# A graph layer in one kernel: score rows computed early, attention maxima moved among the product tiles, and input rows normalized in spans of 4, 4 and 2 tiles

## What is computed

```python
xn = layernorm(x)
# 1. two graph attention convolutions (4 heads of 192, then 2 heads of 96)
h = layernorm(xn) * g + b;  h = h @ W1           # the "first attention product"
s_src, s_dst = (h * a_src).sum(-1), (h * a_dst).sum(-1)      # the scores, per node and head
e = leaky_relu(s_src[src] + s_dst[dst], 0.2)
ee = exp(e - segment_max(e, dst)[dst])
out = segment_sum(ee / segment_sum(ee, dst)[dst] * h[src], dst) + bias
# 2. linear attention with exponential features of keys and queries of xn
# 3. x = x + [x, out2] @ Wu + bu + mix(xn), then a mixture of 8 experts, top 2
```

## Time and profile before

| | us |
|---|---|
| median of 3 runs | 1347.99 |
| the three runs | 1347.99, 1320.34, 1348.22 |
| the profiled execution | 1314.55 |
| its span, first to last instruction | 1312.8 |
| TensorE busy | 1092.2 (83%) |
| VectorE busy | 816.8 (62%) |
| ScalarE busy | 401.0 (31%) |
| GpSimd busy | 306.4 (23%) |

### The profile page before, as it was taken

The page is one execution under the profiler, slowest core; times in us unless marked ns, Lnnn a source line. Parts: engine busy times, 40 slices in busy tenths (PEclk is TensorE's granted clock), DMA queues, the critical chain, the costliest instruction groups (busy, mean ns, idle before and its releaser), DMA issues.

```text
span 1312.8 us, 15580 instructions
## 1 busy us (share of the span) xinstructions
PE 1092.2 (83%) x6105; PEld 975.1 (74%) x6105; DVE 816.8 (62%) x1648; ACT 401.0 (31%) x522; POOL 306.4 (23%) x227
## 2 busy tenths in 40 slices
PE   2999956999999992018999794678699999999998
PEld 1898535667899992018888794677569999999998
DVE  7558993107632595978999668697935433454344
ACT  2443010334100214017666331672242221222211
POOL 1157888888883400010000000000000000000000
PEclk8999985999999996558999897798899999999999
DMA  6926652423555804012000002001010111011103
GB/s 205 312 47 157 127 102 14 72 1 50 118 117 57 238 18 138 0 41 81 1 1 0 1 22 99 0 1 49 1 48 1 48 48 49 1 48 49 49 0 118
DMA packets 67241, 83.14 MB, mean 63 GB/s; under 512 B 31419, under 2 KB 50189, under 8 KB 67169
## 3 DMA queue, kind: packets, MB, share of 16 engines
q1 hardware_dynamic: 37601, 62.27, 15.2%
q0 software_dynamic: 29568, 19.89, 10.1%
HBM read 67.59 MB, written 14.54 MB: 63 GB/s over the span
## 4 chain that ended last, share of the span: by engine, by line
PE 60%; DVE 26%; issue 7%; DMA 3%; ACT 3%; POOL 1%; DVEq 0%; SPq 0%; ACTq 0%; POOLq 0%
PE bank L1280 51%; PE bank L1482 7%; DVE junk_m L1060 7%; DVE junk_k L929 6%; DVE pbuf L1131 3%; DVE pbuf L1105 3%; PE bank L1291 2%; ACT vbuf L762 1%; DVE h L1114 1%; DMA cnt<-table 1%; DVE sb_stats L876 1%; DVE x L1180 1%; DVE sb_stats L877 1%; ACT pbuf L771 1%; DMA keyrow<-key_d 1%
## 5 line engine op out<-in xcount | busy, mean ns | idle before, releaser
L549 POOL DMA_INDIRECT table<-match_n,slot_ix x168 | 277.6, 1652 | 89.6 <-issue 49.7
L1482 PE MATMUL bank<-h,pbuf 128*128 128x193 f32 (+1 forms) x1200 | 190.2, 319 | 31.5 <-DVE pbuf L1131 30.4
L1482 PEld LDWEIGHTS bank<-h,pbuf 128*128 128x128 f32 x1200 | 181.6, 197 | 40.1 <-DVE pbuf L1131 35.9
L1280 PE MATMUL bank<-f_hi,hT 128*128 128x384 f32 x640 | 167.4, 336 | 0.0
L1280 PEld LDWEIGHTS bank<-f_hi,hT 128*128 128x128 f32 x640 | 117.0, 189 | 0.6
L1211 DVE TENSOR_TENSOR hT<-silu,hT 128x512 fp32r<-128x512 f32 (+1 forms) x48 | 28.8, 603 | 141.4 <-ACT hT L825 141.3
L1262 DVE SCALAR_TENSOR_TENSOR x<-bank,sb_gate,x 128x384 f32<-128x384 f32 x160 | 93.5, 613 | 28.9 <-PE bank L1280 28.6
L1280 PE MATMUL bank<-f_lo,hT 128*128 128x384 f32 x320 | 107.7, 337 | 0.0
L1280 PE MATMUL bank<-y2T_hi,f_hi 128*128 128x512 f32 (+1 forms) x288 | 103.2, 358 | 2.9 <-DVE y2T_lo L860 2.9
L929 DVE SCALAR_TENSOR_TENSOR junk_k<-keyrow,key,sb_before 128x384 uint8<-128x384 f32 x168 | 92.8, 614 | 20.1 <-DMA keyrow<-key_d 20.1
L1280 PE MATMUL bank<-y2T_lo,f_hi 128*128 128x512 f32 (+1 forms) x288 | 102.9, 357 | 0.0
(11 more groups left out here) (244 smaller groups left out, 1992.3 us busy)
## 6 DMA issues: line engine op xcount, KB each, us to landing
keyrow<-key_d SPq DMA_DIRECT2D x28, 384.0 KB
table<-zero POOLq DMA_DIRECT2D x2, 3201.0 KB, 28.4
cnt<-table POOLq DMA_DIRECT2D x20, 320.0 KB, 10.9
f_raw<-in_w1T SPq DMA_DIRECT2D x8, 768.0 KB, 4.8
f_raw<-in_w2T SPq DMA_DIRECT2D x8, 768.0 KB, 6.3
w_raw<-in_kqvT SPq DMA_DIRECT2D x4, 1152.0 KB, 7.1
acc_d<-ubuf SPq DMA_DIRECT2D x20, 192.0 KB, 2.1
u_row<-m_d POOLq DMA_DIRECT2D x6, 640.0 KB, 7.8
```

Of the source, the lines that this page charges most:

```text
L549: pool.indirect_dma_start(table[i], bass.IndirectOffsetOnAxis(ap=slot_ix[:, g:g + 1], axis=0), match_n[:, g:g + 1], None, compute_op=ALU.a ...
L1280: return nc.tensor.matmul(o, l, r, start=first, stop=last)
L1482: ins = nc.tensor.matmul(b[:, d * stride:d * stride + chans + 1], score[:, dt * P:(dt + 1) * P], h_t[:, st, h, 0:chans + 1], start=st == 0 ...
```

## The change

- **Spans.** Rows are normalized in spans of 4, 4 and 2 tiles; TensorE turns the second span after key product 0 and the third after key product 2. ScalarE's third square root stands after `channels` of product 2.
- **Second statistics.** Mean 0 and variance `var * rs1 * rs1` are used in place of new `bn_stats`; that root is begun after chunk 1 and used after chunk 12.
- **Loads.** A table gives slot, weights and last use. W1 is loaded whole near the start; key rows 0 and 1 are loaded before the second key half; the 24 small loads of `wk` and `wq` become 6. GpSimd zeroes the tables as soon as x is in, from 388 elements of 16 bits a piece in place of 1067, and table 0 starts at 128 in every entry, so that a count can be read as a bf16 number.
- **Score rows.** `wa` = W1 by `a_src` and `a_dst`: 48 short `tensor_tensor_reduce` on VectorE, three in each of the chunks 3 to 18. In the `u` stage TensorE forms the scores of all nodes from it (`score_rows`, 54 matmuls, bank `sc`) after `bias_rows(0)`, then `score_columns` and `scT`. The 80 `dots` of the `h1` stage and the row_sums go.
- **G copies** and the blocks made from `kvt` and `ksT` move to ScalarE.
- **h1 stage.** ScalarE takes each `h1` tile out (one operation). The low half of W1 is made with g in one operation per block (`split_gain_lo`, 6 short ones). TensorE turns `cnt` itself (no `edge` copy), one mask tile after each of the h1 tiles listed in `PEN_AT`. VectorE runs `masked_max` for mask tiles 0 to 3 with all heads, then tiles 4 to 9 head by head, with `leaky_max` and a transposed row (`max_rows`) for each head. ScalarE takes 128 off `cnt` at the end.
- **Rows of head 0** are loaded like the others; `spread_row` of head 0 goes.

```diff
-        LOADS = [(kT, 0), (kT, 1), (vT, None), (projT, None), (qT, 0), (qT, 1), (Wu[0:D, :], 0), (Wu[0:D, :], 1), (W1, 0), (W1, 1)]
+        LOADS = [(2, kT, 0, None), (1, kT, 1, None), (0, W1, None, None), (2, vT, None, ("k", 0, 2, 2)),
+                 (0, projT, None, None), (1, qT, 0, ("k", 1, 2, KD - 1)), (2, qT, 1, ("kvt",)),
+                 (0, Wu[0:D, :], 0, ("M", 2, 1)), (1, Wu[0:D, :], 1, ("q", 2, KD - 1)),
+                 (2, W1, 0, ("q", 2, KD - 1)), (1, W1, 1, ("u", 1, NT - 1))]
...
+        SPANS = [range(4), range(4, 8), range(8, NT)]
+        SPAN_AT = {0: SPANS[1], 2: SPANS[2]}
...
+        PEN_AT = [(0, 1), (0, 2), (0, 3), (0, 4), (1, 0), (1, 1), (1, 2), (1, 3), (1, 4), (1, 5)]
+        ROWS_AT = {(1, 6): 0, (1, 9): 1}
...
             for c in range(NCH):
                 compare_chunk(c)
                 if c == 1:
                     split_half_lo(dve, K0 + 1)
-                    for t in range(NT):
-                        tile_stats(xrow, t, mv2)
-                    inv_std(mv2, rs2)
+                if c == 1:
+                    step(nc.vector.tensor_tensor(mv2[:, :, 1], mv[:, :, 1], rs1[:, :], ALU.mult))
+                    step(nc.vector.tensor_tensor(mv2[:, :, 1], mv2[:, :, 1], rs1[:, :], ALU.mult))
+                    inv_std_begin(mv2)
...
+                if 3 <= c < 19:
+                    for k, j, h in dot_list[3 * (c - 3):3 * (c - 2)]:
+                        step(nc.vector.tensor_tensor_reduce(
+                            out=junk_d[:, :], in0=w1[:, k, h * C1:(h + 1) * C1], in1=(accb, row_t)[j][:, h * C1:(h + 1) * C1],
+                            scale=1.0, scalar=0.0, op0=ALU.mult, op1=ALU.add, accum_out=wa[:, k, j * H1 + h:j * H1 + h + 1]))
...
+                if c == 20:
                     split_half_lo(dve, Q0)
...
+                    if (hf, t) == (0, 3):
+                        bias_rows(0)
+                        score_rows()
+                    if (hf, t) == (0, 5):
+                        score_columns()
...
                     ins.then_inc(full("h1", hf, t), 1)
-            pe.wait_ge(dots_done, 1)
...
+                    if (hf, t) == (0, 0):
+                        bias_rows(1)
+                    if (hf, t) in PEN_AT:
+                        mask_tile(PEN_AT.index((hf, t)))
+                    if (hf, t) in ROWS_AT:
+                        max_rows(ROWS_AT[hf, t])
+            max_rows(2), max_rows(3)
```

On SP, behind the last stores of the `u` stage:

```diff
+            evacuated(sp, "scT")
+            sp.wait_ge(s_out, 16)
             for i in range(UR):
                 sp.wait_ge(u_out[i], 16 * (2 * NT // UR))
...
+            for h in range(H1):
+                sp.dma_start(a_row[h][:, :], row_of(s_d, h)).then_inc(a_in[h], 16)
+            load_weights(A0 + 1)
```

More of the change, by code:

```diff
@@ L138, in gps_layer @@
         h1 = at("h1", 61440, [P, NT, H1, S1])
[L139 to L144, removed]
@@ L153, in gps_layer @@
[L153 to L157, removed]
+        cnt = [at(f"cnt{i}", SL[0] + 2560 * i if i < 7 else EARLY + 2560 * (i - 7), [P, T], U16) for i in range(NT)]
+        ident_b = at("ident_b", SL[0] + 17920, [P, P], BF16)
@@ L255, in gps_layer @@
                 reserve("kf", *K_MAIN[j - 1])
+            for t in SPAN_AT.get(j, ()):
+                reserve("xT", t, 0), reserve("xT", t, 1)
         reserve("kf", *K_MAIN[-1])
@@ L454, in _ @@
                 if i == UR:
[L455 removed]
+                    load_weights(A0)
                 if i >= 3:
@@ new lines, in _ @@
+            act.wait_ge(rs2_done, 1)
+            for hf in range(2):
+                for t in range(NT):
+                    h1_out(hf, t)
+                    if hf == 0 and t == 3:
+                        split_gain_hi(act, A0 + 1)
+                        weight_rows(1)
+                    if (hf, t) in PEN_AT:
+                        dt = PEN_AT.index((hf, t))
+                        if dt == 4:
+                            finished(act, "h1", 0, NT - 1)
+                        if dt == 0:
+                            for i in range(UR):
+                                act.wait_ge(u_out[i], 16 * (2 * NT // UR))
+                        mask(dt, 0), mask(dt, 1)
@@ L745, in rows_out @@
+            for i in range(NT):
+                nc.scalar.activation(cnt[i][:, :], cnt[i][:, :], ACT.Identity, bias=less_c[:, 0:1]).then_inc(cnt_done, 1)
             def rows_out(stage, k, h, row):
@@ L906, in x_lo @@
                         lo_part(xnT[1][s], transposed(psum("xT", t, h), h), xnT[0][s], "xT", t, h)
-            for tiles in (range(NT // 2), range(NT // 2, NT)):
+            for tiles in SPANS:
                 for t in tiles:
@@ L941, in compare_chunk @@
                                         trash_c[:, :].unsqueeze(1).broadcast_to([P, 2, KW]), ALU.add).then_inc(slots_done, 1)
+            w1 = whole[SLOT[WA]]
+            dot_list = [(k, j, h) for k in range(KD) for j in range(2) for h in range(H1)]
             for c in range(NCH):
@@ L968, in _ @@
-            sums = b[:, 0:MH * M].rearrange("p (g f) -> p g f", g=3)
-            for a in range(4):
-                r = slice(M * a, M * (a + 1))
-                ins = nc.vector.tensor_copy(KD_[r, :, r], sums[r, :, r])
-                ins.then_inc(free("ksT"), 1) if a == 3 else step(ins)
             split_half_lo(dve, Q0 + 1)
@@ new lines, in max_rows, with mask_tile @@
+            def max_rows(h):
+                pe.wait_ge(m_done, h + 1)
+                b = take(pe, "mT", h)
+                nc.tensor.transpose(b[0:2 * NT, 0:P], ucol[:, h, :, :].rearrange("p k t -> p (k t)"), ident[:, :]).then_inc(full("mT", h), 1)
+            def mask_tile(dt):
+                if dt == 0:
+                    pe.wait_ge(cnt_diag, NT)
+                    pe.wait_ge(ident_done, 1)
+                for j in range(2):
+                    b = take(pe, "pen", dt, j).bitcast(BF16)
+                    for i in range(5):
+                        ins = nc.tensor.transpose(b[:, i * P:(i + 1) * P], cnt[5 * j + i].bitcast(BF16)[:, dt * P:(dt + 1) * P],
+                                                  ident_b[:, :])
+                    ins.then_inc(full("pen", dt, j), 1)
```

592 lines of the change are left out of this document (332 added, 260 removed).

## The result

The changed kernel takes 1281.82 us (median of 4 runs, 1281.1 to 1283.0). The kernel before, run beside it, took 1320.1, 1320.3, 1348.0 and 1348.2; its runs fall into two groups some 28 us apart, and the comparison uses the faster one. The ratio is 0.971, with a 95% interval of 0.969 to 0.973. The forecast was 1269, with a range of 1234 to 1302.

A forecast was written before the change was run, and what follows sets the result against it. TensorE, busy for 83% of the span, was taken as the bound, its waits as what can be won. Attention 51.4 us sooner took the span from 1312.8 to 1261.4, execution 1263, plus 5.8 gave 1269 us; range 1234 to 1302.

The forecast's parts named there:

- Step 1: Start of the kernel: key product 0 some 15 us sooner, 4.4 us gained at the end of key features and G.
- Step 2: Wait for G: ScalarE copies G, leaving a 1.2 us wait for the first query half; TensorE's shift becomes -30.6 us.
- Step 3: u stage: 6.6 us wait for the first W1 half, scores added, row_sums gone; shift -10.8 us, ending at 417.45.
- Step 4: Second bias row, behind the first h1 tile: second W1 half lands at 433.15, TensorE waits 12.6 us, bounds 7.4 to 15.5.
- the paragraph on cover: GpSimd's scatters end at 389 and table reads at 411, before TensorE asks at 440; a cover of 29 us.
- Steps 5 and 6: h1 tiles with masks until 502.95, then three more heads' maxima; first attention matmul at 542.8 in place of 594.2.
- The stretch from attention on: From the first attention matmul to the end: left as it is, 718.6 us.
- A: Both W1 halves land in time, without a stall; 27.6 us given back, 1241 us; chance 0.18.
- B: Tables or first query half late, through zeroing, scatters or dots; costs 20 to 25 us, 1292 us; chance 0.16.
- D: VectorE's maxima don't get in among the h1 tiles; gain only about 25 us, 1295 us; chance 0.12.
- C: TensorE stays at its lower clock from the first W1 wait to the last mask; 1350 us and more; chance 0.04.
- The 5.8 us added to the profiled execution: Added to the summed 1263 us because the earlier kernel's profiled execution lay 5.8 below its lowest run; gives 1269.

The follow-up runs named there:

- experiment 6: Changed kernel, one part undone each: all spans ahead of key product 0, 1281.53 us; odd G copies on VectorE, 1283.85; masks behind last h1 tile, 1312.45.
- experiment 3: Changed kernel with the last 24 of 168 scatters left out: 1256.19 us.
- experiment 5: Changed kernel with the 254 filling edges given distinct pairs of unused nodes in place of one repeated pair: 1264.96 us, ratio to before 0.963.
- Experiment 6, third part: Changed kernel with all ten mask tiles and the turns of the maxima behind the last h1 tile: 1312.45 us.
- experiment 8's last kernel: Changed kernel with distinct filling nodes, second W1 half sent ahead of the score rows, its bias row behind h1 tile 3, split behind tile 4: 1247.0 us.
- experiment 4: Changed kernel with the second W1 half's bias row behind h1 tile 6 in place of tile 0, split behind tile 7: 1307.14 us.

## Why the prediction was right, and where it was off

- **Step 1, the start: right.** The first query product, directly behind the key features and `G`, starts at 170.37 in place of 173.47: 3.1 us gained, 4.4 forecast. (The 9 us of experiment 6 are measured against another order, which is slower than the kernel before.) Product 0 came 15.5 us sooner (15 forecast), and the waits of the later spans were 1.2 and 2.9 (3 and 3 forecast).
- **Step 2, `G`: right.** Shift -32.3 for -30.6. The 1.2 us that I had for the first query half did not appear, the products behind `G` took 17.1 us in place of 20.8 (2 had been put down for the clock), and experiment 6 shows that the wait hangs on the copies.
- **Step 3, `u`: right.** The half landed at 321.3 (321.0 forecast); the wait was 8.93 for 6.6 because TensorE came 2.0 us earlier. The stage's shift is -11.1 for -10.8.
- **Step 4, the second W1 half: this one failed.** "So 417.45 + 3.4 + 12.3 = 433.15. TensorE waits 12.6 us." The row shows 34.94. The half landed 22.1 us late. Its first term, 3.4 us from the last `u` tile to the last landed store, measured 8.4; its second, 12.3 us for the rows and the half behind them, measured 29.8. The mechanism of the queue was right: with the slow stretch away the second term is 12.8 (experiment 3) or 12.6 (experiment 5), and the wait 12.3 or 16.4. What failed is the paragraph on cover, "168 of them end at 389, and 20 table reads (about 22 us) at 411". They were sent from 420.2 to 436.9 and landed until 460, over the half's flight. So the load shared the DMA engines with them, which the sum had put at nothing. I had priced the scatters by their pitch on GpSimd, and not by when the last had landed, though the row of `cnt` in the same group, 431.64, could not tell it: there the reads waited for the stores of `u`.
- **Steps 5 and 6, `h1`, masks, heads: right.** From the second bias row to the first attention matmul 106.9 us (forecast 542.8 - 433.15 = 109.7), with the wait of 4.1 for a bank (forecast 4) and heads at a pitch of 10.6. Experiment 6, third part, prices the overlap at 31.9 us.
- **The stretch from attention on: right**, 716.6 for 718.6.
- **Rivals.** A (no stall) is refuted. B did not come by its own sign, a TensorE that waits for `cnt`, nor by its causes, the zeroing or the dots. But the tables were late, complete at 460 in place of 411: the cover that was held against B was not there, and it showed as a longer wait for the half. B's price of 20 to 25 us fits. D did not come. C gave no loss in this kernel beyond the restarts in the sum: the bias rows took 6.61 and 6.23 us, where the second takes 4.03 in experiment 8's last kernel, which has no wait before it. But the mechanism exists, elsewhere: experiment 4 loses 32.9 us to a stage that stays at 1.2 GHz. The Trainium skill (TensorE: Matmul & The Clock Gate, A second HAM failure mode: psum-queue depth-cycling) warns of small idle gaps between groups that throttle the array again and again. What the windows show is unlike it: no gap at all, 8.00 us busy in each 8.00, and the clock low throughout.
- **The 5.8 us added to the profiled execution** had no mechanism, and the changed kernel does not show them: its profiled execution, 1281.1, is 0.7 below the median. That they brought the forecast nearer is luck: the steps alone gave 1263, 18 us too low. The range, drawn to hold D's 1295 as well, held a half that came 22 us late.

The missing 17 us of the span are 22.1 from step 4, less 2.8 from what follows it and 2.0 behind the first attention matmul. Step 4 also explains why undoing the gains of steps 1 and 2 cost so little: until edit 5 the second bias row starts at 454.6, 455.2 or 458.8, whether TensorE comes to it at 429.9, 420.3 or 443.3. What sets it in the first two is GpSimd's chain, scatters, their slow end and the table, which TensorE does not move; only from about 440 on does TensorE's own end of `u`, with the last store and the load behind it, become the later one.

What stays open: why adds onto 256 neighbouring bytes hold up stores of another queue (that they do is shown, not how, and the adds' own packets stay short), and what decides whether TensorE comes back to 2.4 GHz before the `w2` products.

## What to carry to other kernels

When a change moves the busy engine forward, look for the chain that does not move with it, here GpSimd's scatters, and date it by landings, not by sendings: a queue that was never waited for can be 20 us slower than it looks. If undoing a part of a change costs nothing, look at the next wait before calling the part useless: it may have shrunk by just as much. Filling data takes part in the memory traffic; give it addresses as spread as the real ones.

## What the runs showed of the hardware

- 253 adds of 2 bytes in two stretches of 256 bytes: packets of up to 9.3 us on the queue of the loads and stores, a 16 KB instruction fetch of 10.7, a 192 KB store of 22.73, and no add over 1.3. The same number of adds spread out: no packet over 2 us.
- A load of 1152 KB took 5.5 us in the kernel before, 10.4 behind four broadcast rows, 12.7 beside the end of the table reads, 14.4 behind the rows and beside the plain table reads, 19.2 beside all of them, and 27.9 behind the rows and beside all of them.
- One pause, two outcomes: the `w2` products at 75 matmuls in 8 us (granted clock 1.00) or at 40 (0.50), for the whole stage.
